# Step width times input on GpSimd into SBUF, and condition blocks loaded by SyncE, in a selective scan with attention and FFN

## Chip, core and metric

One core of one Trainium2 chip runs the whole program in float32. The metric is the device time of one execution in microseconds (us), as the median of several runs. The engines are named as in the profile: PE is TensorE, DVE is VectorE, ACT is ScalarE, POOL is GpSimd, SP is SyncE.

## What is computed

The reference has two residual parts. The first multiplies each sequence by the weight block that its condition picks, and sends the result through a selective scan; the second is window attention with a routed feed-forward layer. Only the first is touched:

```python
# x [64, 64, 512]: 64 sequences of 64 rows, 512 columns
w = weights[conditions]                        # one 64x64 block per sequence
u = einsum('bct,bcd->bdt', x, w)               # input of the scan
delta = softplus(delta_r @ dt_proj_w.T + dt_proj_b)
dA  = exp(delta[..., None] * A)                # 16 states per channel
dBu = (delta * u)[..., None] * B[:, :, None, :]
h_t = dA_t * h_(t-1) + dBu_t
y_t = einsum('bdn,bn->bd', h_t, C_t) + u_t * D
```

The middle axis (64) is time for the scan and the last one (512) its channels: 64 steps per sequence, each from a zero state.

## The kernel before

`scan_block` computes the first part and, along the way, the keys and queries of the second; `attention_ffn_block` does the rest after it. The engines' programs are written out by hand and meet in semaphores; each engine takes its instructions strictly in order.

**Tiling.** Channels lie on the 128 partitions in four slices (c = 0 to 3), time along the free axis. A tile is 512 tokens, eight sequences (t = 0 to 7, buffers u, delta alternate by h = t % 2), and a tile's four quarters (q = 0 to 3) are two column halves of 256 times two pairs of channel slices. So there are 32 quarters, s = 4t + q. A quarter has eight chunks (k = 0 to 7): one channel slice, four of the 16 states, 256 columns, 1024 elements per partition. A chunk's number is e = 8s + k, 256 in all.

**A chunk's way.** DVE writes delta * u * B into `hid` (`times_b`, L1070), where `du` = delta * u holds two channel slices of 256 columns for the whole quarter and is read as one slice repeated for the four states. ACT writes the decays into PSUM (L722, two buffers). DVE scans in place (L1169). POOL multiplies by C in place (L560). PE adds the four states up with identity matmuls (L1394). `hid` is a ring of five chunk buffers: `times_b` of chunk e waits until PE is done with chunk e - 5.

**du.** Once a quarter DVE computes `du` for the next one (`prepare`, L1083): one multiply of 128x512, from `delta` and `u` in SBUF to PSUM bank 4. It stands between the scans of chunks 6 and 7, since the eighth `times_b` of the quarter is issued before it and must have read the old `du`. On DVE the order is times_b(k+1), scan(k), and at the end prepare, scan(7), times_b(0) of the next quarter.

**Side work.** Once a quarter a group g of 128 tokens (two sequences) is projected, 32 groups in all. `weights` on POOL copies a column of row indices (L472) and gathers 128 rows of `w_cond` by them (L474); `weight_blocks` on ACT copies the two 64x64 blocks on the diagonal of `w_pair` (L643); `project_u` on PE (L1243) multiplies. In quarter s the gather is for group s + 5 and the projection for group s + 4. POOL also has the softplus add (L495, `step`), the key tables (L507), the norms' small products (L481 to L489) and the keys (L517 to L529); the softplus add is there up to quarter 28, twice in quarters 1 and 2, and the rest from quarter 3 on. SP loads and stores; its queue has `store_rows` for the output (L348), then the stores of q (L399) and kv (L402), each behind its waits.

**POOL's order** in a quarter is the eight C multiplies with, after chunk 1 the gather, after 4 the softplus add, after 5 the key tables, after 6 norms and keys.

Of the kernel before, what the change touches and what calls it, by code (L numbers as in the profile page):

```python
# [9 lines left out]
ALU = mybir.AluOpType  # L10
# [3 lines left out]
P = 128  # L14
# [40 lines left out]
FAR = 1.0e6  # L55
MAGIC = 12582912.0
# [33 lines left out]
def scan_block(nc, A, S, W, out):  # L90
# [4 lines left out]
    with ExitStack() as ctx:  # L95
# [8 lines left out]
        du = psum[:, 4, 0:2 * SUB].rearrange("p (c t) -> p c t", c=2)  # L104
# [19 lines left out]
        x1 = [early[1][:].rearrange("p (c t) -> p c t", c=NCH), sb("x1_1", [P, NCH, SUB])]  # L124
        hid = sb("hid", [P, RING, 4, SUB])
# [15 lines left out]
        sq = sb("sq", [P, G + H, HD])  # L141
# [78 lines left out]
        ld_w = [sem(f"ld_w{i}") for i in range(2)]  # L220
        ld_xt = [sem(f"ld_xt{i}") for i in range(2)]
# [10 lines left out]
        dve_du, dve_dbu, dve_h = sem("dve_du"), sem("dve_dbu"), sem("dve_h")  # L232
# [71 lines left out]
        def _(sp):  # L304
            def load_x(g, p):

                wait(sp, pe_u, g - 1)
                sp.dma_start(x_pair[p][:], A["x_pairs"][g]).then_inc(ld_xp[p], 16)

# [57 lines left out]
            def quarter(t, h, q, parts):  # L367
# [21 lines left out]
                if parts.after_scan:  # L389
                    store_rows(s - 1, 0)  # L390
                    store_rows(s - 1, 1)
                if parts.fourth:
                    g, p = s - 3, (q + 1) % 2
                    if s == 4 * NT:
                        sp.wait_ge(dve_lk, 1)
                        store_keys(NG - 3, kvg[(NG - 3) % 2][:])
                    wait(sp, act_q, g + 1)
                    wait(sp, pool_qr, g + 1)
                    sp.dma_start(S["q"][bass.ds(g * GRP, GRP), :], qg[p][:]).then_inc(st_q[p], 16)  # L399
                    if s < 4 * NT:  # L400
                        wait(sp, pool_k, 5 * (g + 1))
                        sp.dma_start(S["kv_new"][bass.ds(g * GRP, GRP), :], kvg[p][:]).then_inc(st_kv[p], 16)  # L402
# [65 lines left out]
        def _(pool):  # L468
# [34 lines left out]

            def key_tables(g):
                wait(pool, pool_k, 5 * g)
                for out, table, i in ((k_cos, cos, 0), (k_sin, sin, 1)):
                    pool.tensor_tensor(  # L507
                        out[:].rearrange("p (a f) -> p a f", a=2),
                        table[:, bass.ds(g * HALF, HALF)].unsqueeze(1).to_broadcast([P, 2, HALF]),
                        one_ks[:, i, :].rearrange("p (a f) -> p a f", a=2), ALU.mult).then_inc(pool_kt, 1)  # L510
# [21 lines left out]
            def gather_first(n):  # L532
# [3 lines left out]
                if n == 0:  # L536
                    pool.wait_ge(dve_du, 4 * (NT - 1))
                    pool.wait_ge(act_exp, 32 * (NT - 1))
                    pool.wait_ge(pe_res, 2 * NCH * (NT - 1))
# [9 lines left out]
            def quarter(t, h, q, parts):  # L549
                s = 4 * t + q  # L550
                for k in range(8):
                    if parts.scan:
                        e, j = 8 * s + k, k % 4
                        r = e % RING
                        if e == 0:
                            pool.wait_ge(ld_first, 16)
                        elif q % 2 == 0 and k in (1 if s == 0 else 0, 2):
                            pool.wait_ge(ld_bc[q // 2][k // 2], 16 * (t + 1))
                        pool.wait_ge(dve_h, e + 1)
                        pool.tensor_tensor(hid[:, r, :, :], hid[:, r, :, :], bc[q // 2][:, 4 * j:4 * j + 4, 1, :],  # L560
                                           ALU.mult).then_inc(pool_hc, 1)
# [3 lines left out]
                    if k == 1:  # L565
# [54 lines left out]
            first_step(1, 0)  # L620
            quarters(pool, quarter)
            for i in range(2):
                pool.wait_ge(ld_w[i], 16 * NG // 2)
# [4 lines left out]
        def _(act):  # L628
# [16 lines left out]
            def take_u(g):  # L645
# [3 lines left out]
                wait(act, dve_du, 2 * before)  # L649
# [10 lines left out]
            def add_bias(g):  # L660
# [4 lines left out]
                wait(act, dve_du, 2 * before)  # L665
# [38 lines left out]
            def quarter(t, h, q, parts):  # L704
# [70 lines left out]
                def query_squares(g, p, heads):  # L775
# [3 lines left out]
                    for i in heads:  # L779
                        nc.scalar.activation(sq[:, G + i, :], qg[p][:, HD * i:HD * i + HD], ACT.Square,  # L780
                                             accum_out=n_ss[:, G + i:G + i + 1]).then_inc(act_ss, 1)

                def key_squares(g, heads):
                    act.wait_ge(act_kv, g + 1)
                    for i in heads:
# [31 lines left out]
                for k in range(8):  # L817
# [7 lines left out]
                    if k == 0:  # L825
                        for g in parts.first[:1]:
                            weight_blocks(g)
# [25 lines left out]
                    if k == 4:  # L853
# [5 lines left out]
                        for g in parts.first[1:]:  # L859
                            weight_blocks(g)  # L860
# [82 lines left out]
        def _(dve):  # L943
# [116 lines left out]
            def times_b(t, h, q, k):  # L1060
# [6 lines left out]
                if k == 0:  # L1067
                    dve.wait_ge(dve_du, 4 * t + q + 1)
# [3 lines left out]

            def prepare(t, h, q):

                if t == q == 0:
                    dve.wait_ge(pool_dh, 2)
                elif q % 2 == 0:
                    dve.wait_ge(pool_dl, 4 * t + q + 2)
                elif t == 0 and q == 1:
                    dve.wait_ge(pool_dl, 2)  # L1080
                wait(dve, dve_dbu, 8 * (4 * t + q))
                at, c = SUB * (q // 2), 2 * (q % 2)
                nc.vector.tensor_tensor(du, delta[h][:, c:c + 2, at:at + SUB], u[h][:, c:c + 2, at:at + SUB], ALU.mult  # L1083
                                        ).then_inc(dve_du, 1)
# [70 lines left out]
            def quarter(t, h, q, parts):  # L1155
# [3 lines left out]
                for k in range(8):  # L1159
                    if k == 7 and parts.next_scan:  # L1160
                        prepare(*after)
# [28 lines left out]
            prepare(0, 0, 0)  # L1190
# [4 lines left out]
        def _(pe):  # L1195
# [39 lines left out]
            def project_u(g):  # L1235
                p = g % 2
                pe.wait_ge(ld_xp[p], 16 * (g // 2 + 1))
                pe.wait_ge(wpair_ok, 2 * (g + 1))
# [1028 lines left out]
```

## Time and profile before

| | us |
|---|---|
| median of 3 runs | 1829.36 |
| lowest and highest | 1827.55, 1831.83 |
| the profiled execution, whole | 1830.78 |
| its span in the trace | 1829.0 |
| DVE, PE, ACT, POOL busy | 1443.5, 1628.9, 1278.7, 1254.2 |
| from 29 to about 900 | the scan's 32 quarters |
| a quarter, 302.2 to 329.3 | 27.10 |
| in it: DVE, POOL, PE, ACT busy | 27.10, 25.81, 23.75, 23.41 |

Busy shares are means over two unlike stages and are read by stage. A row of a timeline has the start, the recorded duration, the engine, the line, output and inputs; two neighbours may overlap by some hundredths, so what an instruction costs its engine is read from start to start. `scan_psum` is any tile in PSUM; `kv_at` and `early` hold one of each pair of buffers (`u`, `delta`, `bc`; `xt`, `x1`). The granted clock is a share of PE's full 2.4 GHz.

### The profile page before, as it was taken

To read this page: it belongs to the slowest core of one execution; us is meant where nothing else is said; L and a number is where in the kernel's file an instruction comes from. 1 tells how busy PE (TensorE), PEld (TensorE's weight loads), DVE (VectorE), ACT (ScalarE), POOL (GpSimd) and SP (SyncE) were. 2 spreads that over 40 slices of the span, in tenths; PEclk is the share of its full clock that TensorE was granted. 3 is DMA by queue.
4 is the path that set the end of the run, shared out by engine and by line. 5 is a ranking of instruction groups with operands and counts; after the bars stand their busy time and mean duration, and the time that the engine had idled before them with its cause. 6 is when DMAs were issued, how large, how long until landed. Compare 5 with 4: busy or idle time off the path is not lost. (4 is left out here: it accounts for less than half of the span.)

```text
span 1829.0 us, 30427 instructions
## 1 busy us (share of the span) xinstructions
PE 1628.9 (89%) x9591; PEld 1135.7 (62%) x9591; DVE 1443.5 (79%) x2542; ACT 1278.7 (70%) x4011; POOL 1254.2 (69%) x1136
## 2 busy tenths in 40 slices
PE   6788888888888888887968799999999999999999
PEld 6666566666565566655535575766657576665755
DVE  8999999999999999999958665655756566575522
ACT  5888888888888888877657675655647565564622
POOL 5789999999999999989867774456454445541010
PEclk9999999999999999998979999999999999999999
DMA  6444344344345335333277663334243234431010
GB/s 219 161 155 152 115 176 163 110 169 164 119 148 181 122 138 181 123 130 124 80 211 200 193 183 86 96 112 127 79 115 99 80 103 113 108 95 43 18 35 12
DMA packets 130039, 230.44 MB, mean 126 GB/s; under 512 B 31496, under 2 KB 82716, under 8 KB 124504
## 3 DMA queue, kind: packets, MB, share of 16 engines
q1 hardware_dynamic: 94456, 158.50, 25.3%
q0 software_dynamic: 35424, 70.00, 14.4%
q8 instruction: 78, 1.28, 0.3%
q14 instruction: 81, 0.66, 0.1%
HBM read 212.88 MB, written 43.65 MB: 140 GB/s over the span
## 5 line engine op out<-in xcount | busy, mean ns | idle before, releaser
L1169 DVE TENSOR_TENSOR_SCAN hid<-scan_psum,hid 128x1024 f32<-128x1024 f32 x256 | 601.7, 2351 | 0.0
L1394 PE MATMUL scan_psum<-ident,hid 128*128 128x128 f32 x2048 | 343.0, 287 | 115.0 <-POOL hid L560 112.6
L1394 PEld LDWEIGHTS scan_psum<-ident,hid 128*128 128x128 f32 x2048 | 256.0, 146 | 272.9 <-POOL hid L560 145.1
L560 POOL TENSOR_TENSOR hid<-hid,kv_at 128x1024 f32<-128x1024 f32 x128 | 306.3, 2406 | 24.0 <-DVE hid L1169 23.5
L560 POOL TENSOR_TENSOR hid<-hid,bc 128x1024 f32<-128x1024 f32 x128 | 305.9, 2402 | 17.8 <-DVE hid L1169 17.4
L1714 ACT COPY p_t<-attn_psum 112x384 f32<-112x384 f32 x256 | 122.1, 483 | 217.9 <-PE attn_psum L2023 217.7
L1852 DVE CUSTOM_DVE_ANT_0 prob<-attn_psum,mask 128x336 f32<-128x336 f32 x256 | 119.8, 505 | 193.3 <-PE attn_psum L2016 192.7
L1599 POOL DMA_INDIRECT kv_at<-in_kv_rows,idx_old x183 | 175.3, 958 | 104.4 <-PE attn_psum L2036 54.1
L1607 POOL DMA_INDIRECT kv_at<-kv_scratch,idx_new x189 | 199.1, 1054 | 61.3 <-issue 56.1
L2104 PE MATMUL attn_psum<-w,ffn_hid 128*128 128x512 f32 x512 | 237.3, 594 | 0.2 <-DVE y_sb L1928 0.2
L2088 PE MATMUL attn_psum<-xs_in,w 128*128 128x256 f32 x1024 | 232.7, 381 | 5.4 <-ACT xs_in L1720 4.3
L722 ACT ACTIVATE scan_psum<-kv_at,neg_a 128x252 f32<-128x252 f32 x512 | 211.3, 462 | 10.4 <-DVE hid L1169 9.3
L722 ACT ACTIVATE scan_psum<-delta,neg_a 128x252 f32<-128x252 f32 x512 | 211.1, 462 | 9.4 <-DVE hid L1169 9.4
L2088 PEld LDWEIGHTS attn_psum<-xs_in,w 128*128 128x128 f32 x1024 | 190.2, 190 | 34.1 <-ACT xs_in L1720 6.2
L1070 DVE TENSOR_TENSOR hid<-scan_psum,bc 128x1024 f32<-128x1024 f32 x128 | 160.5, 1273 | 0.0
L1070 DVE TENSOR_TENSOR hid<-scan_psum,kv_at 128x1024 f32<-128x1024 f32 x128 | 160.1, 1270 | 0.1
L1708 ACT ACTIVATE prob<-prob,ntop 128x336 f32<-128x336 f32 x256 | 148.0, 592 | 6.4 <-DVE ntop L1852 6.1
L1625 POOL DMA_INDIRECT x_rows<-a_scratch,r_idx x16 | 17.7, 1106 | 196.2 <-DVE r_idx L1898 195.9
L1282 PE MATMUL scan_psum<-w_qkv,early 128*128 128x512 f32 x256 | 132.0, 597 | 11.6 <-issue 11.6
L2104 PEld LDWEIGHTS attn_psum<-w,ffn_hid 128*128 128x128 f32 x512 | 89.3, 190 | 74.4 <-issue 73.9
L2023 PE MATMUL attn_psum<-ident,prob 128*112 128x128 f32 x768 | 128.4, 281 | 3.9 <-ACT p_t L1714 3.9
L1282 PE MATMUL scan_psum<-w_qkv,x 128*128 128x512 f32 x224 | 117.3, 606 | 10.0 <-issue 10.0
(231 smaller groups left out, 3033.3 us busy)
## 6 DMA issues: line engine op xcount, KB each, us to landing
bc<-bc_scratch SPq DMA_DIRECT2D x16, 2048.0 KB, 10.0
kv_at<-bc_scratch SPq DMA_DIRECT2D x15, 2048.0 KB, 10.0
q_scratch<-qg SPq DMA_DIRECT2D x32, 260.0 KB, 2.0
early<-q_scratch SPq DMA_DIRECT2D x32, 260.0 KB
x_pair<-in_x_pairs SPq DMA_DIRECT2D x32, 256.0 KB, 4.6
f_wo<-in_w_o SPq DMA_DIRECT2D x32, 256.0 KB, 3.3
out_t<-x_rows SPq DMA_DIRECT2D x64, 128.0 KB, 2.9
a_scratch<-a_sb SPq DMA_DIRECT2D x32, 256.0 KB, 2.6
```

The costliest lines, as they stand in the source:

```text
L560: pool.tensor_tensor(hid[:, r, :, :], hid[:, r, :, :], bc[q // 2][:, 4 * j:4 * j + 4, 1, :], ALU.mult).then_inc(pool_hc, 1)
L722: ex = nc.scalar.activation(decay[k % 2][:, SUB * i:SUB * i + SUB].rearrange("p (b t) -> p b t", t=T)[:, :, 1:T], delta[h][:, c, at:at + S ...
L1070: nc.vector.tensor_tensor(hid[:, e % RING, :, :], du[:, c % 2, :].unsqueeze(1).to_broadcast([P, 4, SUB]), bc[q // 2][:, 4 * j:4 * j + 4, 0 ...
L1169: nc.vector.tensor_tensor_scan(states, decay[k % 2], states, 0.0, ALU.mult, ALU.add).then_inc(dve_h, 1)
L1282: mm = nc.tensor.matmul(pro, x1[b][:, j, at:at + GRP], w_qkv[:, j, D * i:D * i + D], start=(j == 0), stop=(j == NCH - 1))
L1394: mm = nc.tensor.matmul(yc[g], hid[:, e % RING, i, P * g:P * g + P], ident[:], start=False, stop=(k % 4 == 3 and i == 3), is_transpose=Tru ...
L1599: pool.indirect_dma_start(kv[s][:, c, :], None, A["kv_rows"], bass.IndirectOffsetOnAxis(ap=idx_old[:, c, b:b + 1], axis=0)).then_inc(ld_ol ...
L1607: pool.indirect_dma_start(kv[s][:, c, :], None, S["kv_new"], bass.IndirectOffsetOnAxis(ap=idx_new[:, c, NKV * i + s:NKV * i + s + 1], axis=0),
L1708: nc.scalar.activation(prob[u % 4][:], prob[u % 4][:], ACT.Exp, bias=ntop[u % 4][:], scale=-1.0, accum_out=total[u % 4][:]).then_inc(act_e, 1)
L2023: mm = nc.tensor.transpose(p_bank(m, u)[:, P * c:P * c + P], prob[u % 4][:, KC * c:KC * c + KC], ident[:])
L2088: mm = nc.tensor.matmul(h_bank(t, s)[:, FT * i:FT * i + FT], w1[:, c, P * f:P * f + P], xs_in[:, c, :], start=(c == 0), stop=(c == NCH - 1))
L2104: mm = nc.tensor.matmul(y_bank(t, tt), ffn_hid[:, f, P * tt:P * tt + P], w2[:, f, :], start=(f == 0), stop=(f == NF - 1))
```

## The change

There are two parts. First, `du` becomes a tile in SBUF, and POOL computes it, one channel slice (128x256) at a time: slice 0 for the next quarter ahead of its C multiply of chunk 4 (6 in quarter 1), slice 1 ahead of that of chunk 7. DVE's `times_b` waits for slice 0 at chunk 0 and for slice 1 at chunk 4. Second, from group 6 on SP loads the condition's two blocks straight onto the diagonal of `w_pair`, with the block's number read from `ints` into a register; POOL's gather and ACT's copies stay for groups 0 to 5. To make room in SBUF, `sq` shrinks to eight heads and the key squares reuse its slots behind a wait.

```diff
-        du = psum[:, 4, 0:2 * SUB].rearrange("p (c t) -> p c t", c=2)
+        du = sb("du", [P, 2, SUB])
...
+            def load_weights(g, p):
+
+                wait(sp, pe_u, g - 1)
+                for b in range(2):
+                    which = sp.value_load(ints[T * b:T * b + 1, 1 + g:2 + g], min_val=0, max_val=A["w_cond"].shape[0] // HD - 1)
+                    sp.dma_start(w_pair[p][HD * b:HD * b + HD, HD * b:HD * b + HD],
+                                 A["w_cond"][bass.ds(which * HD, HD), :]).then_inc(ld_blk[p], 16)
...
                 if parts.after_scan:
                     store_rows(s - 1, 0)
                     store_rows(s - 1, 1)
+                if s:
+                    for g in parts.gather:
+                        load_weights(g, g % 2)
...
+            def prepare(to, i):
+
+                t, h, q = to
+                s, at, c = 4 * t + q, SUB * (q // 2), 2 * (q % 2) + i
+                if q % 2 == 0 and s:
+                    pool.wait_ge(pool_dl, 4 * t + q + 2)
+                elif s == 1:
+                    pool.wait_ge(pool_dl, 2)
+                wait(pool, dve_dbu, 8 * s - 4 + 4 * i)
+                pool.tensor_tensor(du[:, i, :], delta[h][:, c, at:at + SUB], u[h][:, c, at:at + SUB], ALU.mult
+                                   ).then_inc(pool_du, 1)
...
+                        if k in (6 if s == 1 else 4, 7) and parts.next_scan:
+                            prepare((t, h, q + 1) if q < 3 else (t + 1, 1 - h, 0), k // 7)
                         pool.wait_ge(dve_h, e + 1)
...
-                    if k == 1:
+                    if k == 1 and s == 0:
                         for g in parts.gather[:1]:
                             weights(g, g % 2)
...
+            pool.wait_ge(pool_dh, 2)
+            for i in range(2):
+                prepare((0, 0, 0), i)
...
                 def key_squares(g, heads):
                     act.wait_ge(act_kv, g + 1)
+                    act.wait_ge(act_ss, 12 * g + H)
...
-                            weight_blocks(g)
+                            if g < NPOOL:
+                                weight_blocks(g)
...
-                if k == 0:
-                    dve.wait_ge(dve_du, 4 * t + q + 1)
+                if k % 4 == 0:
+                    dve.wait_ge(pool_du, 2 * (4 * t + q) + k // 4 + 1)
...
-            def prepare(t, h, q):
-
-                if t == q == 0:
-                    dve.wait_ge(pool_dh, 2)
-                elif q % 2 == 0:
-                    dve.wait_ge(pool_dl, 4 * t + q + 2)
-                elif t == 0 and q == 1:
-                    dve.wait_ge(pool_dl, 2)
-                wait(dve, dve_dbu, 8 * (4 * t + q))
-                at, c = SUB * (q // 2), 2 * (q % 2)
-                nc.vector.tensor_tensor(du, delta[h][:, c:c + 2, at:at + SUB], u[h][:, c:c + 2, at:at + SUB], ALU.mult
-                                        ).then_inc(dve_du, 1)
...
-                    if k == 7 and parts.next_scan:
-                        prepare(*after)
...
-                pe.wait_ge(wpair_ok, 2 * (g + 1))
+                if g < NPOOL:
+                    pe.wait_ge(wpair_ok, 2 * (g + 1))
+                else:
+                    pe.wait_ge(ld_blk[p], 32 * ((g - NPOOL) // 2 + 1))
```

On POOL, in the middle of the scan, from one quarter's last C multiply to the next one's seventh. Before:

```order
L560 TENSOR_TENSOR hid<-hid,kv_at 128x1024
L560 TENSOR_TENSOR hid<-hid,bc 128x1024 x2
L472 COPY w_now<-w_idx 128x1
L474 DMA w_rows<-in_w_cond,w_now 128x64
L560 TENSOR_TENSOR hid<-hid,bc 128x1024 x3
L495 TENSOR_TENSOR kv_at<-kv_at,sp_a 128x4x128
L560 TENSOR_TENSOR hid<-hid,bc 128x1024
L507 TENSOR_TENSOR k_cos<-cos,one_ks 128x64
L507 TENSOR_TENSOR k_sin<-sin,one_ks 128x64
L560 TENSOR_TENSOR hid<-hid,bc 128x1024
```

After (L526 is the step multiply, L587 the C multiply, L508 the softplus add, L532 the key tables):

```order
L526 TENSOR_TENSOR du<-delta,u 128x256
L587 TENSOR_TENSOR hid<-hid,kv_at 128x1024
L587 TENSOR_TENSOR hid<-hid,bc 128x1024 x4
L526 TENSOR_TENSOR du<-delta,u 128x256
L587 TENSOR_TENSOR hid<-hid,bc 128x1024
L508 TENSOR_TENSOR kv_at<-kv_at,sp_a 128x4x128
L587 TENSOR_TENSOR hid<-hid,bc 128x1024
L532 TENSOR_TENSOR k_cos<-cos,one_ks 128x64
L532 TENSOR_TENSOR k_sin<-sin,one_ks 128x64
L587 TENSOR_TENSOR hid<-hid,bc 128x1024
```

The copy and the gather are gone from behind the second C multiply, and two step multiplies have come in, ahead of the fifth and of the eighth.

On DVE, around the boundary of two quarters. Before:

```order
L1070 TENSOR_TENSOR hid<-scan_psum,kv_at 128x1024
L1169 SCALAR_TENSOR_TENSOR hid<-scan_psum,hid 128x1024
L1083 TENSOR_TENSOR scan_psum<-kv_at 128x512
L1169 SCALAR_TENSOR_TENSOR hid<-scan_psum,hid 128x1024
L1070 TENSOR_TENSOR hid<-scan_psum,kv_at 128x1024 x2
L1169 SCALAR_TENSOR_TENSOR hid<-scan_psum,hid 128x1024
L1070 TENSOR_TENSOR hid<-scan_psum,kv_at 128x1024
```

After (L1103 is `times_b`, L1187 the scan):

```order
L1187 SCALAR_TENSOR_TENSOR hid<-scan_psum,hid 128x1024
L1103 TENSOR_TENSOR hid<-du,kv_at 128x1024
L1187 SCALAR_TENSOR_TENSOR hid<-scan_psum,hid 128x1024 x2
L1103 TENSOR_TENSOR hid<-du,kv_at 128x1024 x2
L1187 SCALAR_TENSOR_TENSOR hid<-scan_psum,hid 128x1024
L1103 TENSOR_TENSOR hid<-du,kv_at 128x1024
L1187 SCALAR_TENSOR_TENSOR hid<-scan_psum,hid 128x1024
```

The step multiply between the last two scans is gone, and each `times_b` reads `du` where it read `scan_psum`.

On SP, behind the output stores of a quarter, where before the store of q (L399) came next. After:

```order
L358 DMA out_t<-x_rows 128x2x128 x2
L316 TENSOR_LOAD ints
L316 ISA x2
L317 ISA
L317 DMA w_pair<-in_w_cond 64x64
L316 TENSOR_LOAD ints
L316 ISA x2
L317 ISA
L317 DMA w_pair<-in_w_cond 64x64
L412 DMA q_scratch<-qg 128x520
```

Between the two stores stand two register loads, each with its block's DMA.

## Rows read from the trace of the kernel before

**Rows 1.** Page, busy time of each engine; DVE's busy tenths in 40 slices

```profile
PE 1628.9 (89%) x9591; PEld 1135.7 (62%) x9591; DVE 1443.5 (79%) x2542; ACT 1278.7 (70%) x4011; POOL 1254.2 (69%) x1136
...
DVE  8999999999999999999958665655756566575522
```

**Rows 2.** Table of stretches: stretch, length, busy us, granted clock, DMA share, GB/s

```profile
0.00:29.00 29.00, 15.81 (x111) 14.46 (x112) 21.80 (x53) 14.86 (x36) 13.10 (x21) 0.94 0.55 191
...
329.30:871.00 541.70, 453.57 (x2625) 330.79 (x2624) 541.70 (x341) 456.58 (x1597) 513.22 (x454) 0.97 0.41 144
```

**Rows 3.** Timeline of DVE, one quarter: start, us, engine, line, output<-input

```profile
329.31 0.72 DVE L1083 TENSOR_TENSOR scan_psum<-kv_at 128x512 f32<-128x512 f32 x1
329.88 2.34 DVE L1169 TENSOR_TENSOR_SCAN hid<-scan_psum,hid 128x1024 f32<-128x1024 f32 x1
332.08 2.38 DVE L1070 TENSOR_TENSOR hid<-scan_psum,bc 128x1024 f32<-128x1024 f32 x2
...
336.53 1.25 DVE L1070 TENSOR_TENSOR hid<-scan_psum,bc 128x1024 f32<-128x1024 f32 x1
337.64 2.33 DVE L1169 TENSOR_TENSOR_SCAN hid<-scan_psum,hid 128x1024 f32<-128x1024 f32 x1
```

**Rows 4.** Timeline of POOL, the same quarter

```profile
329.52 2.72 POOL L560 TENSOR_TENSOR hid<-hid,bc 128x1024 f32<-128x1024 f32 x1 [0.15 <-DVE hid L1169]
332.20 0.20 POOL L481 TENSOR_TENSOR n_r<-n_r 128x12 f32<-128x12 f32 x1
...
335.85 0.72 POOL L529 TENSOR_TENSOR kvg<-k_n,k_rot 128x256 f32<-128x256 f32 x1
336.53 6.99 POOL L560 TENSOR_TENSOR hid<-hid,bc 128x1024 f32<-128x1024 f32 x3
343.46 0.19 POOL L472 COPY w_now<-w_idx 128x1 int32<-128x1 int32 x1
...
344.94 4.68 POOL L560 TENSOR_TENSOR hid<-hid,bc 128x1024 f32<-128x1024 f32 x2
349.99 2.36 POOL L560 TENSOR_TENSOR hid<-hid,bc 128x1024 f32<-128x1024 f32 x1 [0.37 <-DVE hid L1169]
352.31 1.28 POOL L495 TENSOR_TENSOR delta<-delta,sp_a 128x512 f32<-128x512 f32 x1
...
355.86 0.32 POOL L507 TENSOR_TENSOR k_cos<-cos,one_ks 128x64 f32<-128x64 f32 x1
...
356.62 2.72 POOL L560 TENSOR_TENSOR hid<-hid,bc 128x1024 f32<-128x1024 f32 x1 [0.16 <-DVE hid L1169]
```

**Rows 5.** Timeline of DVE around two step multiplies

```profile
82.94 2.84 DVE L1083 TENSOR_TENSOR scan_psum<-kv_at 128x512 f32<-128x512 f32 x1 [0.40 <-POOL kv_at L495]
85.70 2.28 DVE L1169 TENSOR_TENSOR_SCAN hid<-scan_psum,hid 128x1024 f32<-128x1024 f32 x1
...
112.21 1.00 DVE L1083 TENSOR_TENSOR scan_psum<-kv_at 128x512 f32<-128x512 f32 x1
```

**Rows 6.** Timeline of POOL at the same two places

```profile
82.86 2.37 POOL L560 TENSOR_TENSOR hid<-hid,kv_at 128x1024 f32<-128x1024 f32 x1
...
111.37 1.28 POOL L495 TENSOR_TENSOR delta<-delta,sp_a 128x512 f32<-128x512 f32 x1
112.60 5.25 POOL L560 TENSOR_TENSOR hid<-hid,bc 128x1024 f32<-128x1024 f32 x2
```

**Rows 7.** Single lines of DVE: duration in ns, min/median/max

```profile
L1083 DVE TENSOR_TENSOR scan_psum<-kv_at x16: 674/762/2842, 29.6 to 762.9; 128x512 f32<-128x512 f32 x16
...
L1070 DVE TENSOR_TENSOR hid<-scan_psum,bc x128: 1194/1280/1341, 87.9 to 895.1; 128x1024 f32<-128x1024 f32 x128
```

**Rows 8.** Groups by line, DVE, first 60 us: busy, mean ns, idle

```profile
L1037 DVE TENSOR_TENSOR hid<-pos_f,sheet 128x1024 f32<-128x1024 f32 x1 | 1.2, 1225 | 0.0
```

**Rows 9.** Waits of SyncE's queue, 329 to 871 us: total, times, longest

```profile
SPq L63 <- POOL qg L489: 261.1, 20, 19.7
```

**Rows 10.** DMA issues, 329 to 871 us: count, median us to landing

```profile
w_rows<-in_w_cond,w_now POOLq DMA_INDIRECT x16, 5.6
```

More of the change, by code:

```diff
@@ L55 @@
 FAR = 1.0e6
+NPOOL = 6
 MAGIC = 12582912.0
@@ L140, in scan_block @@
         k_raw = sb("k_raw", [P, G, HD])
-        sq = sb("sq", [P, G + H, HD])
+        sq = sb("sq", [P, H, HD])
         k_n = sb("k_n", [P, G, HD])
@@ L220, in scan_block @@
         ld_w = [sem(f"ld_w{i}") for i in range(2)]
+        ld_blk = [sem(f"ld_blk{i}") for i in range(2)]
         ld_xt = [sem(f"ld_xt{i}") for i in range(2)]
@@ L231, in scan_block @@
         act_exp, act_y, act_kv, act_q = sem("act_exp"), sem("act_y"), sem("act_kv"), sem("act_q")
-        dve_du, dve_dbu, dve_h = sem("dve_du"), sem("dve_dbu"), sem("dve_h")
+        pool_du, dve_dbu, dve_h = sem("pool_du"), sem("dve_dbu"), sem("dve_h")
         act_z, pool_dl = sem("act_z"), sem("pool_dl")
@@ L536, in gather_first @@
                 if n == 0:
-                    pool.wait_ge(dve_du, 4 * (NT - 1))
+                    pool.wait_ge(pool_du, 8 * (NT - 1))
                     pool.wait_ge(act_exp, 32 * (NT - 1))
@@ L620, in _ @@
             first_step(1, 0)
+            pool.wait_ge(pool_dh, 2)
+            for i in range(2):
+                prepare((0, 0, 0), i)
             quarters(pool, quarter)
             for i in range(2):
-                pool.wait_ge(ld_w[i], 16 * NG // 2)
+                pool.wait_ge(ld_w[i], 16 * NPOOL // 2)
             for b in range(NKV2):
@@ L648, in take_u @@
                 act.wait_ge(pe_u, g + 1)
-                wait(act, dve_du, 2 * before)
+                wait(act, pool_du, 4 * before)
                 wait(act, pe_res, NCH * before)
@@ L664, in add_bias @@
                 wait(act, pool_dl, g - 1)
-                wait(act, dve_du, 2 * before)
+                wait(act, pool_du, 4 * before)
                 wait(act, act_exp, 16 * before)
@@ L779, in query_squares @@
                     for i in heads:
-                        nc.scalar.activation(sq[:, G + i, :], qg[p][:, HD * i:HD * i + HD], ACT.Square,
+                        nc.scalar.activation(sq[:, (G + i) % H, :], qg[p][:, HD * i:HD * i + HD], ACT.Square,
                                              accum_out=n_ss[:, G + i:G + i + 1]).then_inc(act_ss, 1)
@@ L859, in quarter @@
                         for g in parts.first[1:]:
-                            weight_blocks(g)
+                            if g < NPOOL:
+                                weight_blocks(g)
                         if parts.fourth:
@@ L1189, in _ @@
             place_tokens()
-            prepare(0, 0, 0)
             times_b(0, 0, 0, 0)
@@ L1237, in project_u @@
                 pe.wait_ge(ld_xp[p], 16 * (g // 2 + 1))
-                pe.wait_ge(wpair_ok, 2 * (g + 1))
+                if g < NPOOL:
+                    pe.wait_ge(wpair_ok, 2 * (g + 1))
+                else:
+                    pe.wait_ge(ld_blk[p], 32 * ((g - NPOOL) // 2 + 1))
                 if g > 1:
```

## Prediction

> **What bounds the kernel now.** I read the page's busy times and DVE's 40 slices first. The reader is to see two halves: VectorE (DVE) stands at 8 and then 9 up to about 900 us and mostly at 5 to 7 after that, where TensorE (PE), 89% busy in all, takes over [rows 1]. The table of stretches says the same in numbers: from 329.3 to 871 us DVE is busy 541.7 of 541.7 us, GpSimd (POOL) 513.2, PE 453.6, ScalarE (ACT) 456.6 [rows 2]. All that the change touches lies in this first half, the scan, so the second half keeps its length, and I price the scan alone.
>
> Then the timeline of one quarter, DVE's rows first [rows 3]. The reader is to see a loop with no hole: a times-B multiply (L1070) goes to the next scan in 1.11 to 1.12 us, a scan (L1169) to the next instruction in 2.20, and the step multiply (L1083) takes 0.57 us from its start to the next one's. A quarter is 8 x (1.12 + 2.20) + 0.57 = 27.1 us, and POOL's rows repeat after 27.10. Then POOL's rows of the same quarter [rows 4]: it idles only 0.37 + 0.16 us, waiting for a scan. DVE is the bound, and POOL is 0.5 us a quarter behind it.
>
> **Two-input DVE instructions and POOL.** L1083 is the only DVE instruction inside the scan loop with both inputs in SBUF. Three places show what that means while POOL works. At 329.31 L1083 starts first, and the C multiply (L560) that starts at 329.52 takes 2.72 us where the others take 2.34 to 2.36: it stood 0.36 us until L1083 had read [rows 3, 4]. At 82.94 POOL was first: L560 runs 82.86 to 85.23 at its usual 2.37, and L1083 takes 2.84 us, ending at 85.78, 0.55 us after POOL [rows 5, 6]. At 112.21 L1083 comes in the middle of a softplus add that ends at 112.65; L1083 ends at 113.21, again 0.56 us later, and the two L560 behind take 5.25 us for 4.7: the waiting DVE went ahead of POOL's next instruction [rows 5, 6]. So the two exclude one another, first come first served, in turn. L1070, with du in PSUM, shows nothing of it: 128 of them lie between 1.19 and 1.34 us (the other 128, with the other buffer, alike), although POOL works beside nearly all of them [rows 7].
>
> **What the change does to L1070.** du moves from PSUM to SBUF, so all 256 times-B multiplies get two SBUF inputs, as L1083 has now. Alone they keep their length: the angle multiply L1037 with the same size and two SBUF inputs took 1.225 us, L1070 has a median of 1.28 [rows 7, 8]. Beside POOL they must take turns with it. The Trainium skill has this rule ("SBUF — State Buffer", Who interferes with whom): a DVE instruction with two SBUF inputs contends with a GpSimd instruction that reads SBUF, and whichever starts first keeps the shared ports for its whole instruction; it speaks against this change. The three places agree with its direction.
>
> **The sum for a steady quarter.** POOL's time in the traced quarter is 329.52 to 356.62 = 27.10 us [rows 4]. Less idle 0.53, less the 0.36 stood behind L1083, less the gather of weight rows (343.46 to 344.94 = 1.48 us, which SyncE takes over from group 6 on): 24.73. Added are two step multiplies of 128x256; the k add of that size (L529) goes to the next instruction in 0.68 us and lasts 0.72, I take 0.70 each: 26.13. Every one of POOL's remaining instructions reads SBUF. DVE needs its turn 8 times for 1.12 us: 9.0. If each turn excludes the other wholly, a quarter is 26.1 + 9.0 = 35.1 us. But the turns overlap a little: L1083 ended 0.55 us after POOL although it takes 0.68 alone [rows 5, 7], so 0.13 us of each of 8 turns lie under POOL's end: 34.0 us. DVE's own work is 26.5, so it is no longer the bound; the shared reading is, and it costs 34.0 - 27.1 = 6.9 us a quarter. The ring of five hid buffers lets DVE run up to four chunks ahead of POOL, which hides waits of the moment but not a mean demand above the period.
>
> By the skill's rule taken to the letter (same page and section), exclusion for the whole instruction, it would be 35.1 us a quarter; the trace's 0.55 us speaks for slightly less.
>
> **Over the scan.** Quarters 3 to 28 have this mix: 26 x 6.9 = 179. Quarters 29 to 31 have no softplus add (L495, 1.28 us in the row, 1.23 to the next start) and the last prepares no successor: 32.8 - 27.1 = 5.7 twice and 4.3 once, 16. Quarters 0 to 2 have no key work (332.20 to 336.53, and the two tables from 355.86 on, 0.6; 4.9 us), but one more softplus add or weight gather: 26.1 - 4.9 + 1.3 + 9.0 - 1.05 = 30.4, so 3.3 each, 10. Sum 205. The profiled execution took 1830.8 us against a span of 1829.0 and a median of 1829.4; 1829 + 205 = **2034 us**.
>
> **The other parts.** Step multiply taken from DVE: 32 x 0.57 = 18.2 us, plus the two collisions (at 82.94: 2.76 to the next scan and 0.40 idle before; at 112.21: 0.3 more), 2.9: 21 us [rows 3, 5]. This gain is inside the sum, because DVE's 26.5 is compared with 34.0. It would come through only if the exclusion did not. Waits for du: the halves are made before POOL's chunks 4 and 7 and needed by DVE at the next quarter's chunks 0 and 4, and DVE may not be more than four chunks ahead by the ring anyway: nothing of its own. What is queued behind a waiting multiply on DVE is the scan, and behind that POOL's C multiply, ACT's exponentials and PE's sums.
> SyncE's load: per quarter two register loads and two issues of 16 KB, in its queue behind the output stores and ahead of the q store. That q store waits right there for POOL, 261.1 us in 20 quarters or 13 us each [rows 9], so the four instructions would have to cost over 13 us to move anything. The register load has no row; its landing is bounded by 0 and the 5.6 us of POOL's gather [rows 10], and PE needs the block only in the next quarter. I take 0. ACT loses 52 copies and gets one wait on its own counter; it was busy 456.6 of 541.7 us [rows 2]: 0. The first two step multiplies, on POOL ahead of the first chunk, cost 2 x 0.70 where DVE took 0.57: under 1 us, left out.
>
> **Rivals.**
> First, the exclusion doesn't reach L1070: its first input is a 256-column row repeated four times, and if only a second full stream goes the shared way, L1070 stays at 1.12 a turn. Then DVE's 26.5 is the bound, POOL's 26.1 fits below it, and the gain above comes through: 1829 - 21 = **1808 us**. The sign turns at 0.57 / 8 = 0.07 us of waiting per multiply: less is faster, more is slower. For it: no traced two-input instruction beside POOL has a repeated input. Against: L1083's delay lasted to POOL's end, and B, the second input of L1070, is itself a full stream.
> Second, the exclusion is partial: POOL's multiply of 2.4 us for 1024 columns leaves gaps, and a long two-input DVE instruction shares them. Half the cost gives 1829 - 21 + 0.5 x 226 = **1921 us**. Against: L1083 at 82.94 got nothing for over 2.2 us.
> Third, the same exclusion with PE as a further bound. PE was busy 453.6 of 541.7 us, 22.7 a quarter, at a granted clock of 0.97 [rows 2]; in 34 us that is 67%. If the grant fell to the lower level (1.2 GHz) for long, its work would come near 45 us a quarter, and the time near **2380 us**: 31 x 17.9 = 555 more. Against: over the first 29 us PE was busy only 54% at 0.94 [rows 2].
>
> **Chances.** Forecast (full turns, 2000 to 2070) 0.84; first rival 0.07; second 0.06; third 0.03. The range holds both ends of the turn's price: no overlap at all, 35.1 us, adds 33 us (2067); twice the overlap takes 33 off (2001). A measurement of this kernel can tell about 0.2% from no change. Faster 0.07, the same 0.01, slower 0.92.
>
> **What the profile after would show.** Right: times-B multiplies with du from SBUF, their mean well above 1.28 us and single ones up to about 3.5; POOL's C multiply at 2.36 in some and about 3.4 in many; a quarter of 34 us; DVE and POOL both short of full by their mutual waits only; 26 gathers gone from POOL; PE idle more behind POOL; nothing changed after the scan. Wrong: times-B multiplies still at 1.2 to 1.3 us; a quarter of 26.5; or long waits of PE for the SyncE blocks, or of DVE for du. A quarter of 34 us with PE's clock at half would mean that I have the right number for another reason.

## The result and the profile after

The changed kernel takes 2028.7 us (median of 4 runs, 2024.2 to 2029.7), against 1828.5 us (median of 4, 1826.4 to 1831.8) for the kernel before. The ratio is 1.109, with a 95% interval of 1.107 to 1.111: about 200 us slower. The profiled execution has a span of 2022.5 us.

The page of the kernel after, busy time of each engine, then the busy tenths and PE's granted clock in 40 slices; beside [rows 1]:

```profile
PE 1681.8 (83%) x9591; PEld 1175.3 (58%) x9591; DVE 1627.5 (80%) x2510; ACT 1265.9 (63%) x3959; POOL 1491.6 (74%) x1148
...
DVE  8999999999999999999998686656565656565622
...
POOL 6899999999999999999999677654545444443010
PEclk8998989888988898989779789999999999999999
```

The scan now fills 22 slices. DVE is busy 184 us more and POOL 237 us more, although DVE has 32 instructions fewer and POOL only 12 more: both stay longer in the same instructions. A busy DVE at 9 in every slice hides this, since an instruction that waits inside itself counts as busy.

The table of stretches (length, busy us of PE, PEld, DVE, ACT, POOL, granted clock, DMA share, GB/s), beside [rows 2]:

```profile
330.00:1065.00 735.00, 539.16 (x2873) 396.00 (x2874) 725.71 (x350) 489.21 (x1712) 724.19 (x500) 0.87 0.34 116
```

POOL is busy 724 of 735 us, and it is never idle for long; PE and ACT have room.

Single lines of the kernel after: durations in ns, min/median/max. L1103 is the times-B multiply, beside L1070 in [rows 7]; L587 is the C multiply:

```profile
L1103 DVE TENSOR_TENSOR hid<-du,kv_at x128: 1192/1299/5633, 29.4 to 1023.2; 128x1024 f32<-128x1024 f32 x128
L1103 DVE TENSOR_TENSOR hid<-du,bc x128: 1192/1298/5554, 94.2 to 1094.7; 128x1024 f32<-128x1024 f32 x128
```
```profile
L587 POOL TENSOR_TENSOR hid<-hid,kv_at x128: 2337/2358/3371, 34.5 to 1038.8; 128x1024 f32<-128x1024 f32 x128
```

The fastest multiply is as fast as ever (1.19 us), the median hardly moved, and the mean (page, L1103) rose from 1.27 to 1.94 and 2.02 us. Only the spread tells the story: some go straight through, others wait.

One quarter on DVE (start, us, engine, line), beside [rows 3]:

```profile
600.79 3.32 DVE L1103 TENSOR_TENSOR hid<-du,kv_at 128x1024 f32<-128x1024 f32 x1
604.03 2.28 DVE L1187 TENSOR_TENSOR_SCAN hid<-scan_psum,hid 128x1024 f32<-128x1024 f32 x1
606.23 1.19 DVE L1103 TENSOR_TENSOR hid<-du,kv_at 128x1024 f32<-128x1024 f32 x1
607.75 2.29 DVE L1187 TENSOR_TENSOR_SCAN hid<-scan_psum,hid 128x1024 f32<-128x1024 f32 x1 [0.33 <-ACT scan_psum L752]
609.96 3.08 DVE L1103 TENSOR_TENSOR hid<-du,kv_at 128x1024 f32<-128x1024 f32 x1
```

and on POOL, beside [rows 4]:

```profile
600.00 0.72 POOL L526 TENSOR_TENSOR du<-kv_at 128x256 f32<-128x256 f32 x1
600.68 14.57 POOL L587 TENSOR_TENSOR hid<-hid,kv_at 128x1024 f32<-128x1024 f32 x5
615.22 1.72 POOL L526 TENSOR_TENSOR du<-kv_at 128x256 f32<-128x256 f32 x1
...
619.22 2.25 POOL L508 TENSOR_TENSOR delta<-delta,sp_a 128x512 f32<-128x512 f32 x1
...
633.64 0.72 POOL L526 TENSOR_TENSOR du<-kv_at 128x256 f32<-128x256 f32 x1
```

The multiply at 600.79 came 0.11 us after POOL's C multiply, waited for it and ended at 604.11. The one at 606.23 came 0.05 us before the next C multiply, went straight through, and the C multiply stood still for it. POOL's row of five C multiplies takes 14.57 us where five took 11.7 [rows 4]: three turns. Its step multiply takes 1.72 instead of 0.72, the softplus add 2.25 instead of 1.28: one turn each, about 1.0 us, a little less than the 1.12 us that a times-B multiply has from start to start. The step multiply at the head of the row comes back after 633.64 - 600.00 = 33.64 us: that is the quarter now.

### The profile page after: what moved, and what is told of

It is laid out like the page before. It is cut to its first block and busy times, and to the rows that moved or that the text cites. A ratio compares the mean times of both kernels' runs of the same rounds, so it can differ in the third digit from the quotient of the medians.

```text
span 2022.5 us, 30748 instructions
## 1 busy us (share of the span) xinstructions
PE 1681.8 (83%) x9591; PEld 1175.3 (58%) x9591; DVE 1627.5 (80%) x2510; ACT 1265.9 (63%) x3959; POOL 1491.6 (74%) x1148
## 3 DMA queue, kind: packets, MB, share of 16 engines
q8 instruction: 78, 1.28, 0.3%
## 5 line engine op out<-in xcount | busy, mean ns | idle before, releaser
L1187 DVE TENSOR_TENSOR_SCAN hid<-scan_psum,hid 128x1024 f32<-128x1024 f32 x256 | 580.4, 2276 | 17.1 <-ACT scan_psum L752 17.1
L1414 PE MATMUL scan_psum<-ident,hid 128*128 128x128 f32 x2048 | 372.6, 308 | 254.7 <-POOL hid L587 252.9
L1414 PEld LDWEIGHTS scan_psum<-ident,hid 128*128 128x128 f32 x2048 | 276.9, 157 | 426.7 <-POOL hid L587 301.0
L587 POOL TENSOR_TENSOR hid<-hid,kv_at 128x1024 f32<-128x1024 f32 x128 | 347.9, 2734 | 10.1 <-DVE hid L1187 9.6
L587 POOL TENSOR_TENSOR hid<-hid,bc 128x1024 f32<-128x1024 f32 x128 | 349.1, 2743 | 2.2 <-DVE hid L1187 1.5
L1103 DVE TENSOR_TENSOR hid<-du,kv_at 128x1024 f32<-128x1024 f32 x128 | 257.0, 2017 | 2.2 <-POOL du L526 2.2
L1103 DVE TENSOR_TENSOR hid<-du,bc 128x1024 f32<-128x1024 f32 x128 | 247.7, 1944 | 0.4 <-PE scan_psum L1414 0.4
```

Source lines behind the costliest of these rows:

```text
L1103: nc.vector.tensor_tensor(hid[:, e % RING, :, :], du[:, c % 2, :].unsqueeze(1).to_broadcast([P, 4, SUB]), bc[q // 2][:, 4 * j:4 * j + 4, 0 ...
L1187: nc.vector.tensor_tensor_scan(states, decay[k % 2], states, 0.0, ALU.mult, ALU.add).then_inc(dve_h, 1)
L1414: mm = nc.tensor.matmul(yc[g], hid[:, e % RING, i, P * g:P * g + P], ident[:], start=False, stop=(k % 4 == 3 and i == 3), is_transpose=Tru ...
```

## Experiments

Each kernel was timed beside the kernel before on the same chip. The experiments ran on three chips, and the kernel before took 1826.7 to 1827.4 us on them, so that times of different experiments can be compared to within a few us. A "turn" is the time in which POOL stands still while a DVE instruction with two SBUF inputs reads, or the other way round; "plain turns" means that they alternate and nothing else costs. The question for the first four was whether the 200 us come from the place of `du`, from POOL's added work, or from SyncE's loads.

### SyncE's loads alone

```diff
+                if s:
+                    for g in parts.gather:
+                        load_weights(g, g % 2)
...
-                    if k == 1:
+                    if k == 1 and s == 0:
```

> The kernel before with only the second part of the change: SyncE loads the condition's blocks from group 6 on, POOL's gather and ACT's copies stay for groups 0 to 5; the step multiply stays on DVE with du in PSUM. Theory of turns (POOL and a DVE instruction with two SBUF inputs take turns, and nothing else costs): DVE keeps its 27.1 us a quarter, so no change, 1826 to 1831 us; POOL has 1.5 us a quarter more idle time. Rival, the register loads and their DMAs hold up SyncE's queue or PE: slower, up to the whole 200 us of the change if they are its cause.

Measured: 1828.5 us, ratio 1.0006 (0.9995 to 1.0018). The loads cost nothing. Table of stretches of this kernel:

```profile
330.00:870.00 540.00, 454.39 (x2621) 332.24 (x2620) 540.00 (x339) 446.00 (x1563) 493.79 (x421) 0.96 0.42 144
```

DVE is busy 540.0 of 540.0 us; POOL's busy time fell by some 18 us against [rows 2] and bought nothing.

### du in SBUF, all else as before

```diff
-        du = psum[:, 4, 0:2 * SUB].rearrange("p (c t) -> p c t", c=2)
+        du = sb("du", [P, 2, SUB])
...
-        sq = sb("sq", [P, G + H, HD])
+        sq = sb("sq", [P, H, HD])
```

> The kernel before with only du's place changed from PSUM to SBUF (and sq shrunk to make room, as in the change); DVE still computes du in one 128x512 multiply, POOL still gathers. Theory of turns: all the cost is here. The changed kernel's quarter is 33.64 us; less POOL's two step multiplies 1.40, plus DVE's own turn 0.57, plus the gather 1.48 if it counts as a turn: 34.3 us, 2048 us in all; if DVE can work under the gather, 32.8 us, about 2003 us. Rival, POOL is simply overloaded by the step multiplies or DVE waits for them: POOL has none here, so no change, 1829 us.

Measured: 2095.1 us, ratio 1.146 (1.144 to 1.148). The place of `du` alone makes the kernel slower by more than the whole change does, with no instruction added to POOL. So the rival of an overloaded POOL is out. (This kernel also has the smaller `sq` and ACT's wait for it; the fourth experiment has both too and is fast.) But the size missed: 47 us above the 2048 us of plain turns. The trace shows a pattern that the theory did not have. POOL of this kernel, around a gather (L474):

```profile
623.38 2.00 POOL L474 DMA_INDIRECT w_rows<-in_w_cond,w_now  x1 [0.27 <-DVE hid L1170]
625.40 6.98 POOL L560 TENSOR_TENSOR hid<-hid,kv_at 128x1024 f32<-128x1024 f32 x3
632.33 1.28 POOL L495 TENSOR_TENSOR kv_at<-kv_at,sp_a 128x512 f32<-128x512 f32 x1
636.98 3.24 POOL L560 TENSOR_TENSOR hid<-hid,kv_at 128x1024 f32<-128x1024 f32 x1 [3.37 <-DVE hid L1170]
```

and DVE:

```profile
627.16 7.54 DVE L1071 TENSOR_TENSOR hid<-du,kv_at 128x1024 f32<-128x1024 f32 x1
```

This multiply came while the first of three C multiplies ran, let all three and the softplus add pass, and ended 1.09 us after the add, at 634.70. Then POOL had nothing to do for 3.37 us. The gather itself took 2.00 us; its median is 1.99 us in this kernel and 1.00 in the kernel before, so it too can stand still for a multiply. Elsewhere in the same kernel a waiting multiply mostly gets in after one POOL instruction (177 of 256). Multiplies that let four POOL instructions pass occur 20 times, always as the first behind a gather; in the changed kernel, which has no weight gathers behind group 5, none does.

### du in SBUF and SyncE's loads

This is the kernel above with the loads of the first experiment, so the changed kernel except that DVE computes `du`.

> du in SBUF, computed by DVE, and SyncE's loads: the changed kernel except that DVE computes du. Theory of turns: 33.64 - 1.40 + 0.57 = 32.8 us a quarter, 27 us less than the changed kernel, about 2002 us; the difference to the kernel with du's place alone is what the gather costs, 1.48 x 26 = 38 us if it takes a turn, 0 to 12 if not. Rival of the overloaded POOL: 1829 us, or less.

Measured: 2008.4 us, ratio 1.099 (1.098 to 1.101), 6 us above the 2002 expected. Its steady quarter is 32.8 us by its scans' starts, as expected. Against the changed kernel it is 20 us faster: computing `du` on POOL costs two turns of 0.7 us, on DVE one of 0.57. Against the kernel with gathers it is 87 us faster, where a plain turn would give 38.

### The same POOL work, du handed back to PSUM

```diff
-        du = sb("du", [P, 2, SUB])
+        du = psum[:, 4, 0:2 * SUB].rearrange("p (c t) -> p c t", c=2)
+        du_s = sb("du_s", [P, 2, SUB])
...
-                        if k in (6 if s == 1 else 4, 7) and parts.next_scan:
-                            prepare((t, h, q + 1) if q < 3 else (t + 1, 1 - h, 0), k // 7)
+                        for i in (range(2) if k == (6 if s == 1 else 3) and parts.next_scan else ()):
+                            prepare((t, h, q + 1) if q < 3 else (t + 1, 1 - h, 0), i)
...
+            def take_du(s):
+
+                act.wait_ge(pool_du, 2 * s + 2)
+                wait(act, dve_dbu, 8 * s)
+                nc.scalar.copy(du, du_s[:]).then_inc(act_du, 1)
...
+                    if k == 7 and parts.next_scan:
+                        take_du(s + 1)
```

> The changed kernel with POOL computing du in SBUF ahead of its fourth C multiply, and ACT copying it (128x512, one copy a quarter, 0.6 us) into PSUM bank 4 during DVE's last two scans of the quarter, from where the times-B multiplies read it as before. POOL has all the work it has in the changed kernel. Theory of turns: no DVE instruction of the loop has two SBUF inputs, so DVE's quarter is 8 x 3.32 = 26.5 us: 1829 - 21 = 1808 us, range 1804 to 1816. Rival of the overloaded POOL: its work is the same as in the changed kernel, so 2029 us or a little more.

Measured: 1815.7 us, ratio 0.994 (0.992 to 0.995). POOL does all it does in the changed kernel, and the 200 us are gone; 11 us of the possible 21 come through. This is the kernel that beats both. ACT's copy takes 0.56 us and stands behind a row of exponentials:

```profile
613.24 1.64 ACT L759 ACTIVATE scan_psum<-delta,neg_a 128x252 f32<-128x252 f32 x4
614.82 0.56 ACT L680 COPY scan_psum<-du_s 128x512 f32<-128x512 f32 x1
```

The times-B multiplies read PSUM again and are even (groups by line, 330 to 860 us; busy, mean ns), and by its scans' starts a quarter takes 26.5 us in about 20 of 31 cases and up to 27.2 in the rest:

```profile
L1113 DVE TENSOR_TENSOR hid<-scan_psum,bc 128x1024 f32<-128x1024 f32 x80 | 95.0, 1197 | 0.0
```

DVE waits 1.9 us for ACT in that stretch. By the traces the scan is 16 us shorter than before and starts 1 us later.

### POOL computes du and keeps the gather

```diff
-                    if k == 1 and s == 0:
+                    if k == 1:
                         for g in parts.gather[:1]:
                             weights(g, g % 2)
...
-                if s:
-                    for g in parts.gather:
-                        load_weights(g, g % 2)
```

> The first part of the change alone: POOL computes du into SBUF, and POOL also keeps the gather of weight rows for all 32 groups. Against the changed kernel, POOL has 1.48 us more in 26 quarters. Theory of plain turns: 26 x 1.48 = 38 us more than the changed kernel's 2029, 2067 us. Theory from the run with du's place alone, where the first times-B multiply after a gather took 7.5 to 8.5 us and let three C multiplies and the softplus add pass (a gather costs DVE its place in the turns until POOL runs out of ready work): that run lay 87 us above the one without gathers, so 2029 + 87 = 2116 us, with such long multiplies once a quarter.

Measured: 2114.8 us, ratio 1.157 (1.155 to 1.159). Plain turns (2067) are out; the gather costs 86 us here as it did 87 there. So the SyncE loads, worth nothing alone, are worth 86 us once `du` is in SBUF. One place of this kernel, on POOL (gather L484, C multiply L584, step multiply L523):

```profile
515.34 2.01 POOL L484 DMA_INDIRECT w_rows<-in_w_cond,w_now  x1 [0.27 <-POOL w_now L482]
517.37 4.68 POOL L584 TENSOR_TENSOR hid<-hid,kv_at 128x1024 f32<-128x1024 f32 x2
522.00 1.72 POOL L523 TENSOR_TENSOR du<-delta,u 128x256 f32<-128x256 f32 x1
```

and on DVE:

```profile
518.59 4.55 DVE L1100 TENSOR_TENSOR hid<-du,kv_at 128x1024 f32<-128x1024 f32 x1
```

Here the multiply behind the gather let two C multiplies pass and got in ahead of the step multiply, though POOL was not idle. "Until POOL runs out of ready work", as the expectation had it, is therefore not the rule. Nor is it over with that multiply. The next one, with no gather in between, came while the C multiply that starts at 523.68 ran, let three POOL instructions pass and got in ahead of the key table at 529.54, which took 1.29 us for 0.31:

```profile
525.26 5.39 DVE L1100 TENSOR_TENSOR hid<-du,kv_at 128x1024 f32<-128x1024 f32 x1
```
```profile
526.00 1.26 POOL L505 TENSOR_TENSOR kv_at<-kv_at,sp_a 128x512 f32<-128x512 f32 x1
527.22 2.35 POOL L584 TENSOR_TENSOR hid<-hid,kv_at 128x1024 f32<-128x1024 f32 x1
529.54 1.29 POOL L529 TENSOR_TENSOR k_cos<-cos,one_ks 128x64 f32<-128x64 f32 x1
530.79 0.31 POOL L529 TENSOR_TENSOR k_sin<-sin,one_ks 128x64 f32<-128x64 f32 x1
532.93 2.36 POOL L584 TENSOR_TENSOR hid<-hid,kv_at 128x1024 f32<-128x1024 f32 x1 [1.83 <-DVE hid L1184]
```

A multiply of 5.4 us stands there in each of 23 quarters on end, and POOL then waits 1.83 us for a scan.

### The gather in another place

In the kernel with only du's place changed, the gather stands behind the softplus add of chunk 4.

```diff
-                    if k == 1:
+                    if k == 1 and s == 0:
                         for g in parts.gather[:1]:
                             weights(g, g % 2)
...
+                    if k == 4 and s:
+                        for g in parts.gather[:1]:
+                            weights(g, g % 2)
```

> du in SBUF computed by DVE, gather on POOL, as in the run of 2095 us, but the gather stands behind POOL's softplus add of chunk 4 and no longer behind the C multiply of chunk 1, where POOL had three chunks ready to multiply. The work of every engine is the same. Plain turns, or a gather that costs by its length: 2095 us again. Lost place until POOL is idle: POOL waits for a scan soon after that add, so the lost time shrinks, 2040 to 2065 us, and no times-B multiply passes four POOL instructions.

Measured: 2051.8 us, ratio 1.123 (1.121 to 1.125), 43 us faster with the same work. So the extra cost is not that of the gather's length. Against the kernel without gathers (2008.4 us) 43 us are left, near the 38 us of 26 gathers taken at their length. The letter of the expectation holds for times-B multiplies, but the lost place went to another instruction: in this kernel the first two-input instruction behind the gather is DVE's step multiply (L1087), and it waits 5.5 us. DVE:

```profile
606.67 6.20 DVE L1087 TENSOR_TENSOR du<-kv_at 128x512 f32<-128x512 f32 x1
```

POOL beside it:

```profile
606.07 1.00 POOL L474 DMA_INDIRECT w_rows<-in_w_cond,w_now  x1 [0.27 <-POOL w_now L472]
607.10 2.35 POOL L560 TENSOR_TENSOR hid<-hid,kv_at 128x1024 f32<-128x1024 f32 x1
609.41 0.32 POOL L507 TENSOR_TENSOR k_cos<-cos,one_ks 128x64 f32<-128x64 f32 x1
609.69 0.31 POOL L507 TENSOR_TENSOR k_sin<-sin,one_ks 128x64 f32<-128x64 f32 x1
609.97 2.35 POOL L560 TENSOR_TENSOR hid<-hid,kv_at 128x1024 f32<-128x1024 f32 x1
612.28 0.65 POOL L481 TENSOR_TENSOR n_r<-n_r 128x12 f32<-128x12 f32 x1
```

It came 0.60 us after the gather's start, while only the gather ran, and still waited for the four POOL instructions behind it. What is missing here is the idle time: from 330 to 900 us POOL of this kernel never waited for a scan, where it waited 47.2 us in the kernel of 2095 us and 27.4 us in that of 2115 us.

### POOL writes where it multiplied

The C multiply is left out; POOL writes zeros into the same chunk.

```diff
-                        pool.tensor_tensor(hid[:, r, :, :], hid[:, r, :, :], bc[q // 2][:, 4 * j:4 * j + 4, 1, :],
-                                           ALU.mult).then_inc(pool_hc, 1)
+                        pool.memset(hid[:, r, :, :], 0.0).then_inc(pool_hc, 1)
```

> The changed kernel with POOL's C multiply left out: in its place POOL writes zeros into the same chunk of hid (a memset, which reads nothing from SBUF); so the scan's output lacks all states. Times-B multiplies still have two SBUF inputs. If DVE takes turns with what POOL reads: POOL's reading work is 26.1 - 18.8 = 7.3 us a quarter and DVE has 26.5 of its own, so it is bound by DVE with a few waits, 26.6 to 28 us a quarter, 1808 to 1855 us, and times-B multiplies that start beside a memset take 1.2 us. If a POOL instruction that only writes also excludes them, those are stretched to the memset's end. If the two-input form were slow by itself, the time stays near 2029 us.

Measured: 1828.2 us, ratio 1.0006 (0.9993 to 1.0019), a quarter of 27.1 us. That it equals the kernel before is chance: DVE no longer makes `du`, which would give 26.5 us, and about 0.6 us a quarter goes into waits for what POOL still reads (60 of the 256 times-B multiplies took more than 1.23 us). Two SBUF inputs by themselves cost nothing, as the durations show. Side by side, POOL:

```profile
617.90 0.96 POOL L587 MEMSET hid<- 128x1024 f32 x1 [2.37 <-DVE hid L1186]
...
621.21 0.95 POOL L587 MEMSET hid<- 128x1024 f32 x1 [1.67 <-DVE hid L1186]
```

and DVE:

```profile
617.76 1.20 DVE L1102 TENSOR_TENSOR hid<-du,kv_at 128x1024 f32<-128x1024 f32 x1
...
621.07 1.20 DVE L1102 TENSOR_TENSOR hid<-du,kv_at 128x1024 f32<-128x1024 f32 x1
```

Each memset starts 0.14 us after a times-B multiply, and neither is stretched: all 256 memsets took 0.94 to 0.97 us. Of the 256 multiplies, 166 had only a memset beside them (up to their last 0.15 us), and these took 1.19 to 1.22 us. It is POOL's reading that excludes them, not its writing. The Trainium skill says so ("SBUF — State Buffer", Who interferes with whom): a DVE instruction with two SBUF inputs contends with a GpSimd instruction that reads SBUF, not with one that only writes it. The trace agrees, with these 166.

### Every step multiply twice

```diff
+                pool.tensor_tensor(du[:, i, :], delta[h][:, c, at:at + SUB], u[h][:, c, at:at + SUB], ALU.mult
+                                   ).then_inc(pool_x, 1)
+                pool.wait_ge(pool_x, 2 * s + i + 1)
```

> The changed kernel with each step multiply on POOL done twice, the second behind the first's end: 0.8 us more of POOL's reading, twice a quarter, same result. Theory of turns (the sum of POOL's reading and DVE's two-input time is the bound): every added microsecond shows, 31.5 x 1.6 = 50 us, 2079 us. If DVE or PE were the bound, or POOL had slack: unchanged, 2029 us.

Measured: 2076.7 us, ratio 1.136 (1.134 to 1.138). It is 48 us above the changed kernel for some 50 us of added reading on POOL: nearly every microsecond shows, though DVE got nothing more to do.

### The best kernel with the gather kept

The kernel of 1816 us with the gather on POOL and no SyncE loads (the diff of the gather kept, above).

> The kernel of 1816 us (POOL computes du, ACT copies it to PSUM) with POOL's gather kept for all groups and no SyncE loads. No two-input DVE instruction in the loop, so no turns; POOL's own work is 26.1 + 1.5 = 27.6 us a quarter, above DVE's 26.5, so POOL becomes the bound: about 27.6 us in 24 quarters, 1816 + 24 x 1.0 = 1840 us (1830 to 1846). This tells what the SyncE loads are worth: nothing where DVE is the bound, 24 us here. Rival, the gather hides in POOL's idle time: 1816 us.

Measured: 1834.7 us, ratio 1.0056 (1.0034 to 1.0077). It lies in the expected range: a quarter is 27.5 us in most cases, and POOL, with 0.4 us of waiting for scans in 330 to 860 us, is the bound. So here SyncE's loads are worth about 19 us, as plain work taken from POOL.

### The index copy without the gather

In the kernel with du in SBUF, computed by DVE, and SyncE's loads, POOL makes only the copy of the row index, with the gather's wait.

```diff
+                    if k == 1 and s:
+                        for g in parts.gather:
+                            pool.tensor_copy(w_now[g % 2][:], w_idx[:, bass.ds(g, 1)]).then_inc(wnow_ok, 1)
+                            wait(pool, wnow_ok, g + 1)
```

> The kernel of 2008 us (du in SBUF computed by DVE, SyncE loads) plus POOL's index copy of 128x1 once a quarter behind the C multiply of chunk 1, with the wait for its own end that the gather had, and no gather. It splits the 87 us between that kernel and the one with gathers (2095). If the copy with its wait did it: near 2095 us. If the gather's DMA instruction does: the copy costs its 0.45 us at most, 26 x 0.45 = 12 us or less, 2008 to 2020 us, and no DVE instruction lets more than two POOL instructions pass.

Measured: 2017.6 us, ratio 1.105 (1.103 to 1.106): 9 us for the copy and its wait, so 78 of the 87 us hang on the gather's DMA instruction.

## Why the prediction was right, point by point

**The cause.** Forecast: times-B multiplies take turns with POOL's reading as L1083 did. The place of `du` alone gives 2095 us, the same POOL work with `du` in PSUM 1816 us, the two-input form beside a POOL that mostly writes 1828 us. The first rival (the repeated row escapes) and the second (partial exclusion, 1921 us) are out.

**The quarter.** Forecast 34.05 us: POOL 26.1, eight turns of 0.99 each. Measured 33.64. Seen from POOL, from start to start, a turn cost 0.98 to 1.01 us beside large instructions (3.34 against 2.35, 1.72 against 0.72) and 0.85 to 0.98 in the chains of small ones, probably because POOL's own gap between two dependent instructions runs under the turn. The eight turns of the quarter at 600 us come to 7.7 us where the forecast had 7.9; the other 0.15 us or so is POOL's own work. The higher figure of the prediction, 35.1 us for exclusion over the whole instruction, is out by 1.5 us.

**The sum.** By the starts of chunk 0's scans, the first four quarters took 125.7 us against 112.0 before, 13.7 more (forecast 17); the 25 after them 33.65, 6.55 more each, 164 (forecast 6.9 each, 172); the last three 7.3, 5.7 and the rest more, in all 23 (forecast 16). The forecast for these three left out a piece of POOL's work that both kernels have: seven gathers of K and V rows (L570), of 0.96 to 1.79 us each, which were hidden before, when DVE was the bound. Also, DVE waited 8.2 us for ACT's decays between 998 and 1101 us, and one multiply behind such a gather took 5.55 us. How the 7 us divide among these is not shown. The scan as a whole, from the first times-B multiply to the last scan's end, went from 870.3 to 1070.9 us: 201 against the 205 of the sum. That it is so near is in part luck: the first quarters and the steady ones were 11 us too dear, the last ones 7 us too cheap.

**The second half.** "Keeps its length" was off by 6 us in the profiled execution: 928.3 us after the last scan before, 922.2 after, with the same instructions. In the other kernels it lies between 922 and 928 without an order that I could find. The medians differ by 200.3 us, which fits either way. This stays open.

**The other parts.** SyncE's loads: forecast 0, measured 1.0006. That is what the loads themselves cost in the kernel before, and in the changed kernel no engine is seen to wait for their blocks from 330 to 1060 us. What they replace is another matter: added to the first part of the change alone, they save 86 us. The prediction had the gather as 1.48 us of POOL's time, 38 us for 26 of them. That was too cheap by more than a factor of two with the gather behind the C multiply of chunk 1, and near the 43 us measured with it behind the softplus add. "In turn" as a rule also fails behind gathers. Since the change removes nearly all of them, the sum was spared. Waits for `du`: DVE waited once, 2.2 us at the start.

**The third rival** (PE's clock). The granted clock of the scan did fall, from 0.97 to 0.87 in the mean of the long stretch, and PE's identity matmul went from 287 to 308 ns in the mean. The fall had the rival's direction and not its size, and PE did not become the bound: it was busy 539 of 735 us, and DVE waited for it 0.4 us in the whole scan. ACT did wait for PE (54.1 us in the largest group from 330 to 1060 us), but had room; DVE's waits for ACT came to 8.8 us there.

## What to carry to other kernels

An operand's place can be part of a schedule: here each DVE instruction with both inputs in SBUF took turns with POOL's instructions that read SBUF, so before a buffer is moved from PSUM to SBUF, add the lengths of the two engines' readings and compare the sum, not each engine, with the period. Work can still be moved to POOL if a third engine with room hands the result back to PSUM; that turned 200 us lost into 11 gained. And look at the spread of an instruction's duration, not at its median, and at busy time with suspicion, when two engines take turns.

## What the runs showed that was not expected

**A gather costs DVE its turn.** Behind a weight gather on POOL the first two-input DVE instruction mostly let two to four more POOL instructions pass (durations of 4.55, 6.20 and 7.54 us for 1.19, 0.66 and 1.19 us alone), where otherwise one passed; in the kernel of 2115 us the second did so too (5.39 us). The gathers cost 87 and 86 us in two pairs of kernels, where 26 of them with their copies would be 38 by their length, and 43 us in another place of POOL's order; without the DMA instruction the long multiplies were gone. In both dear kernels POOL stood idle for a scan after the long multiplies, 3.37 and 1.83 us a time, and in the one of 43 us it did not. So a lost turn seems to cost where it leaves POOL without work; that is read from the traces and no run was made for it. By what rule the turn comes back is open: in one kernel when POOL idled, in two others ahead of a step multiply and of a norm product.

**The turn is not always taken at the next instruction in the changed kernel either.** Three of its 256 times-B multiplies let two POOL instructions pass and took 5.2 to 5.6 us: at 44.9 and 66.2 us, in the quarters in which POOL still issues gathers, and at 1083.7 us, in one of the last quarters, where POOL prefetches K and V rows by gathers. The prediction had expected at most about 3.5 us. Each is the first multiply behind a gather, and the steady quarters, without gathers, have none. But the multiplies behind the other six K/V gathers of the scan let at most one instruction pass, so a gather alone does not bring it about; no run tested these places.
